# Rounding two feed-forward weights to bf16 in SBUF and turning them by DMA, with the first projections and the first LayerNorm regrouped

## The chip, the cores and the metric

One core of a Trainium2 chip runs the whole kernel. The metric is the device time of one execution in microseconds (us), taken as the median of the runs. TensorE (PE) does the matrix products, VectorE (DVE), ScalarE (ACT) and GpSimd (POOL) the rest, and SyncE (SP) issues nearly all DMAs.

## What is computed

For a batch of 8 sequences of 512 rows and 512 columns: LayerNorm, cross attention to 120 context rows with 16 heads, a residual, then a feed-forward net whose two weights are quantized to the values -1, 0 and 1 times one scale each.

```python
def weight_quant(w):
    scale = 1.0 / jnp.clip(jnp.mean(jnp.abs(w)), 1e-05)
    q = jnp.clip(jnp.round(w * scale), -1.0, 1.0) / scale
    return w + stop_gradient(q - w)
def bitlinear(x, w, b):
    return einsum('bsd,fd->bsf', act_quant(rmsnorm(x)), weight_quant(w)) + b
x = x + attn(layernorm(x), ctx, ctx, mask)      # softmax(q k^T / sqrt(32)) v, then wo
h = gelu(bitlinear(layernorm(x), w1, b1))       # w1: 2048 x 512
x = x + bitlinear(h, w2, b2)                    # w2: 512 x 2048
```

The scale needs the mean of |w| over a whole weight before any part of it can be rounded, and TensorE needs each weight turned (the contracted dimension on the partitions).

## The kernel before

**Tiles and slots.** The rows are cut into 32 tiles of 128 (k), four to a sequence (b). Every engine runs its own hand-written list of 128 slots (n), four to a tile. In slot n the softmax of one group of four heads of tile n // 4 is done: `softmax_max` on DVE (mask and negative maximum), `exps(n - 1)` on ACT, `normalize(n - 2)` on POOL, `turn_probs(n - 3)` on PE and `evac_probs(n - 3)` on ACT. `scores(n // 4)` fills four PSUM banks, ps_s, in every fourth slot. The later steps of tile k follow at fixed distances: `attend` at slot 4k + 7, `project_out` at 4k + 9, `residual` at 4k + 10, `ln2_scales` at 4k + 11, `ffn_up` from 4k + 14 on, `ffn_down` at 4k + 22. Semaphores tie the lists together; each engine works strictly in its list's order.

**A batch ahead.** TURNS and PROJ say in which slots the next sequence is prepared: "c" and "x" are turns of the context and of the four column blocks of the normalized input, "k", "v" and "q" the projections. All projections and `attend` and `project_out` share one PSUM bank, ps_a, so each waits until the last user of that bank has been read. STATS_AT and LN1_AT are the slots of LayerNorm 1, of which DVE does the statistics (`ln1_stats`) and POOL the factors and the application.

**The start.** Before slot 0 SP issues the loads, PE turns the first context and input and projects keys and the four blocks of queries of sequence 0. In `first_q` the three parts of an exact product are done one after another because wq_l comes late; `project_q` then does the other three blocks (12 matmuls each), and `evac_q` on ACT empties ps_a between them.

**The feed-forward weights** arrive in eight pieces of 128 x 2048 fp32 (p; m = p // 4 says which weight). They borrow buffers: pieces 0 and 1 hid, 2 and 3 the space of w2T, 4 that of q_hT, 5 the first four tiles of x2 (`stage`, after wo has left it), 6 and 7 hid again. What is done with each:
- `sum_abs`: four on ACT (L716, into w_abs) and four on DVE (L918).
- `total_weights` (L530, slots 1 and 7): a small matmul that sums over partitions. `weight_scales` on DVE (slots 2 and 8) makes mean, inverse and scale.
- `round_piece`: w times the inverse plus a magic number, then clipped: two passes on DVE (L925, L928) for even j, two on POOL (L1144, L1147) for odd j, in slots ROUND_AT.
- `turn_piece` on PE (L547, slots TURN_AT = 3 to 6 and 9 to 12): 16 fp32 transposes a piece, four to a bank, alternating between ps_z and ps_y; `evac_piece` on ACT (L727) and on DVE (L939) takes the magic number off and writes bf16 into w1T or w2T, two each per piece. ps_y is also the bank of the turns of TURNS.

`ffn_up` waits at its first call for w1T, `ffn_down` for w2T. SP frees the borrowed buffers in order: load_piece(6) and (7) wait for turned pieces, load_residual(2) for piece 5.

Of the kernel before, what the change touches and what calls it, by code (L numbers as in the profile page):

```python
# [27 lines left out]
def xattn_bitffn_kernel(nc, x, ctx_in, mask, wq, bq, wk, bk, wv, bv, wo, bo, w1, b1, w2, b2, out):  # L28
# [73 lines left out]
    for n in range(NU):  # L102
# [24 lines left out]
    with ExitStack() as stack:  # L127
# [30 lines left out]
        w_deq = sb("w_deq", [P, 2])  # L158

# [56 lines left out]
        names += [f"piece{p}_in" for p in range(8)]  # L216
# [40 lines left out]
        def _(sp):  # L257
# [33 lines left out]
            def slot(n):  # L291
                if n == 2:
                    sp.wait_ge(s["wo_split"], 1)
                    load_piece(5)
                if n == 4:
                    sp.wait_ge(s["wT_full"], 4)
                    load_piece(6)
                if n == 5:
                    sp.wait_ge(s["wT_full"], 8)
# [66 lines left out]
        def _(pe):  # L366
            def wait_free(use):
# [124 lines left out]
            def ffn_up(k, c):  # L492
                j = FC * k + c
                if j == 0:
                    pe.wait_ge(s["wT_act"], 16)
# [36 lines left out]
            def turn_piece(j, quarters):
                p = TURN[j]
                if j % 2 == 0:
                    pe.wait_ge(s["w_ready_dve"], j // 2 + 1)
                else:
                    pe.wait_ge(s["w_ready_pool"], j // 2 + 1)
                for q in quarters:
                    if q % 2 == 0:
                        wait(pe, "wT_act", 2 * j + q // 2)  # L540
                        bank = ps_z
                    else:
                        wait_free(Y[Y_N[("m", j, q)] - 1])
                        bank = ps_y
                    for c in range(4):
                        col = c * D + q * P if p < 4 else (4 * q + c) * P
# [690 lines left out]
```

## Time and profile before

| | us |
|---|---|
| median of 3 runs | 765.94 |
| lowest and highest of them | 760.66, 766.47 |
| the profiled execution, whole | 764.71 |
| its span, first to last instruction | 762.9 |

Mean granted TensorE clock 0.968 of full speed. The page of the profile gives each engine's busy time; the timeline and the chain of waits give the order of events, and the stretches (windows) give busy time between two instants. The span is what the rows cover; 1.8 us lie around it.

### The profile page before, as it was taken

The numbers are of one execution on the slowest core, as the hardware profiler recorded it, in microseconds if no ns is written. First come the engines' busy times: TensorE is split into PE (matmuls) and PEld (weight loads), VectorE is DVE, ScalarE is ACT, GpSimd is POOL, SyncE is SP. The second block draws the span as 40 slices with busy tenths as digits, with TensorE's granted clock in tenths as the row PEclk, the third lists the DMA queues.
The fourth block names the chain that finished last, engine by engine and source line by source line (L and its number), as shares of the span: only waits on it lengthen the run. The fifth ranks groups of instructions, "written<-read, shape, count | busy, mean of one in ns | idle before, by whom it ended". The sixth has DMA issues, their size and how long they took to land.

```text
span 762.9 us, 13877 instructions
## 1 busy us (share of the span) xinstructions
PE 666.9 (87%) x4856; PEld 428.1 (56%) x4856; DVE 604.4 (79%) x1060; ACT 521.7 (68%) x1455; POOL 505.8 (66%) x645
## 2 busy tenths in 40 slices
PE   7756778989999999999999999999999998887885
PEld 5434566656666556556655666656655664554432
DVE  3396776789788897889887978889788778888783
ACT  2254544797578778877687767877888878777360
POOL 3056343776867777777777687767777768777664
PEclk9978889999999999999999999999999999999998
DMA  9933012043322421243334332252223233232244
GB/s 308 378 123 125 12 37 69 22 104 76 76 49 57 125 51 53 64 118 76 76 63 118 76 77 57 55 122 57 54 52 74 66 63 63 63 63 64 56 77 110
DMA packets 109204, 65.37 MB, mean 86 GB/s; under 512 B 90775, under 2 KB 90775, under 8 KB 108495
## 3 DMA queue, kind: packets, MB, share of 16 engines
q1 hardware_dynamic: 108079, 64.49, 33.8%
q8 instruction: 39, 0.64, 0.3%
q14 instruction: 30, 0.25, 0.1%
q10 hardware_dynamic: 1056, 0.00, 0.1%
HBM read 35.12 MB, written 8.39 MB: 57 GB/s over the span
## 4 chain that ended last, share of the span: by engine, by line
PE 36%; DVE 35%; ACT 16%; issue 5%; DMA 4%; POOL 3%; SPq 1%; ACTq 0%; DVEq 0%; POOLq 0%
PE ps_a L405 13%; PE ps_z L507 5%; DVE hid L870 5%; DVE yw L854 5%; ACT prob L693 5%; PE ps_y L522 4%; PE ps_a L435 4%; PE ps_a L478 3%; ACT hid L700 3%; DVE yq L857 2%; PE ps_t L466 2%; DVE bn L849 2%; DVE nmax L834 2%; DVE ps_s L831 2%; DVE oT_l L799 2%
## 5 line engine op out<-in xcount | busy, mean ns | idle before, releaser
L1106 POOL TENSOR_TENSOR prob<-prob,pinv 128x480 f32<-128x480 f32 x128 | 126.3, 987 | 177.5 <-DVE pinv L839 177.5
L693 ACT ACTIVATE prob<-ps_s,nmax 128x120 f32<-128x120 f32 x512 | 180.2, 385 | 34.5 <-DVE nmax L834 34.1
L507 PE MATMUL ps_z<-w1T,q_xT 128*128 128x512 bf16 x476 | 123.9, 383 | 5.6 <-DMA q_xT<-q_x 4.5
L870 DVE SCALAR_TENSOR_TENSOR hid<-ps_z,y_deq,b_row 128x512 f32<-128x512 f32 x119 | 88.6, 744 | 45.3 <-PE ps_z L507 45.3
L693 ACT ACTIVATION_READ_ACCUMULATOR prob<-ps_s,nmax 128x1 f32 x512 | 118.2, 231 | 0.0
L522 PE MATMUL ps_y<-w2T,q_hT 128*128 128x512 bf16 x480 | 114.1, 382 | 0.3 <-DMA q_hT<-xn 0.3
L831 DVE COPY_PREDICATED_SCALAR ps_s<-hidden_key,masked_c 128x480 f32 x128 | 89.5, 700 | 16.4 <-PE ps_s L456 16.4
L466 PE MATMUL ps_t<-ident,prob 128*120 128x128 f32 x512 | 79.2, 278 | 18.0 <-ACT probT L665 10.9
L834 DVE TENSOR_REDUCE nmax<-ps_s 128x4 f32<-128x480 f32 x128 | 84.1, 657 | 4.4
L665 ACT COPY probT<-ps_t 120x512 f32<-120x512 f32 x128 | 79.5, 621 | 7.6 <-PE ps_t L466 7.2
L466 PEld LDWEIGHTS ps_t<-ident,prob 128*120 128x120 f32 x512 | 59.8, 139 | 40.4 <-ACT probT L665 21.3
L522 PEld LDWEIGHTS ps_y<-w2T,q_hT 128*128 128x128 bf16 x480 | 46.2, 99 | 62.1 <-issue 12.1
L1113 POOL TENSOR_SCALAR hid<-hid,hs 128x2048 f32<-128x2048 f32 x31 | 61.0, 1969 | 25.9 <-ACT q_h L708 18.7
L672 ACT ACTIVATE qT<-ps_a,bq_col 128x512 f32<-128x512 f32 (+1 forms) x32 | 19.7, 615 | 84.8 <-PE ps_a L405 80.5
L877 DVE TENSOR_REDUCE hs<-hid 128x1 f32<-128x2048 f32 x32 | 72.8, 2275 | 0.0
L700 ACT ACTIVATE hid<-hid 128x2048 f32<-128x2048 f32 x32 | 61.2, 1913 | 11.3 <-DVE hid L870 10.9
L507 PEld LDWEIGHTS ps_z<-w1T,q_xT 128*128 128x128 bf16 x476 | 43.0, 98 | 45.5 <-issue 13.2
L405 PE MATMUL ps_a<-xnT_h,wq_h 128*128 128x512 f32 x124 | 53.5, 431 | 15.7 <-DVE oT_l L799 11.9
L1120 POOL TENSOR_SCALAR q_h<-hid 128x2048 bf16<-128x2048 f32 x30 | 58.7, 1955 | 2.6
L405 PE MATMUL ps_a<-wo_h,oT_h 128*128 128x512 f32 x128 | 57.6, 450 | 2.4 <-DVE oT_l L799 1.4
L708 ACT ACTIVATE q_h<-hid 128x2048 bf16<-128x2048 f32 x28 | 54.2, 1937 | 0.0
L405 PE MATMUL ps_a<-wo_l,oT_h 128*128 128x512 f32 x128 | 51.4, 401 | 0.0
(155 smaller groups left out, 1397.6 us busy)
## 6 DMA issues: line engine op xcount, KB each, us to landing
xn<-in_x_dram SPq DMA_DIRECT2D x8, 1024.0 KB, 5.7
x<-in_x_dram SPq DMA_DIRECT2D x32, 256.0 KB, 2.7
out_dram<-x SPq DMA_DIRECT2D x32, 256.0 KB, 3.2
hid<-in_L_ffn_w_dram SPq DMA_DIRECT2D x4, 1024.0 KB, 8.8
w2T<-in_L_ffn_w_dram SPq DMA_DIRECT2D x2, 1024.0 KB, 14.0
ctx_k<-in_ctx_dram SPq DMA_DIRECT2D x8, 240.0 KB, 4.0
ctx_k<-in_mask_Bx1xSxS_ik_dram SPq DMA_DIRECT2D x7, 240.0 KB, 2.8
wk_s<-in_L_xattn_wk_dram SPq DMA_DIRECT2D x1, 1024.0 KB, 8.6
```

Source lines behind the costliest of these rows:

```text
L405: last = nc.tensor.matmul(bank, w, m, start=(k == 0 and i == 0), stop=(k == KD - 1 and i == 2))
L466: last = nc.tensor.transpose(ps_t[0:S2, g * P:(g + 1) * P], prob[:, n % 3, g * S2:(g + 1) * S2], ident[:])
L507: last = nc.tensor.matmul(bank[:], q_xT[:, k % 3, i], w1T[:, i, c * CH:(c + 1) * CH], start=(i == 0), stop=(i == KD - 1))
L522: last = nc.tensor.matmul(y_bank(k)[:], q_hT[:, k % 2, f], w2T[:, f], start=(f == 0), stop=(f == KF - 1))
L665: nc.scalar.copy(probT[0:S2, i], ps_t[0:S2, :].rearrange("p (g q) -> p g q", g=G)).then_inc(s["p_evac"], 1)
L693: last = nc.scalar.activation(prob[:, n % 3, g * S2:(g + 1) * S2], ps_s[n % HG][:, g * S2:(g + 1) * S2], ACT.Exp, bias=nmax[:, n % 4, g:g ...
L700: nc.scalar.activation(hid[:, k % 2], hid[:, k % 2], ACT.Gelu).then_inc(s["gelu_done"], 1)
L831: v.copy_predicated(sc, hidden_key[:, k // T % 2, k % T].unsqueeze(1).to_broadcast([P, G, S2]), masked_c[:].unsqueeze(2).to_broadcast([P, ...
L834: v.tensor_reduce(out=nmax[:, n % 4], in_=sc, op=ALU.max, axis=AX_X, negate=True).then_inc(s["sc_max"], 1)
L870: v.scalar_tensor_tensor(hid[:, k % 2, c * CH:(c + 1) * CH], z_bank(FC * k + c)[:], y_deq[:, k % 8:k % 8 + 1], b1_row[:, c * CH:(c + 1) * ...
L877: v.tensor_reduce(out=hs[:, 3, t:t + 1], in_=hid[:, k % 2], op=ALU.max, axis=AX_X, apply_absolute_value=True).then_inc(s["h_abs"], 1)
L1106: gp.tensor_tensor(pr, pr, pinv[:, n % 4].unsqueeze(2).to_broadcast([P, HG, S2]), ALU.mult).then_inc(s["prob_ready"], 1)
```

## The change

1. `round_piece` on DVE no longer multiplies and clips in fp32. It compares: w < -mean/2 into a bf16 buffer, then (w > mean/2) minus that, a `scalar_tensor_tensor`, in the same buffer w_t[:, 0] (even pieces). Odd pieces: `clip_piece` does two passes on POOL (times, min; max, plus magic), and `round_piece` on ACT takes the magic number off into w_t[:, 1] as bf16.
2. The turn of a piece is one transposing DMA from w_t (128 x 2048 bf16), issued by SP in slots TURN_W_AT. All TensorE transposes and PSUM evacuations of the weights go. w1T is stored as [P, 16, 4, 128], so that `ffn_up` reads its 512 moving columns as four runs of 128 with a step of 512 elements.
3. `first_q` and the `project_q` of sequence 0 get a bank each (ps_a, ps_s[1], ps_s[2], ps_s[3]).
4. The first input is loaded as four DMAs, and LayerNorm 1 of sequence 0 is done in halves.
5. Order: all sums of the first weight, `total_weights(0)` and `weight_scales(0)` come before slot 0; the second total is in slot 8 (it was in 7, its scales in 8). Piece 3 is loaded ahead of wv. load_piece(6) waits for round_piece(0), load_piece(7) for ACT's first rounding, load_residual(2) for ACT's third. Turns of sequence 1: 2 c, 4 to 7 x, 8 k (were 3, 5, 6, 7, 9, and 8); projections 3 k, 6 v, 9, 10, 12, 14 q (were 5, 6, 10, 12, 13, 14).

```diff
-            turns = {3: ("c", 0), 5: ("x", 0), 6: ("x", 1), 7: ("x", 2), 8: ("k", 0), 9: ("x", 3)}
-            proj = {5: ("k", 0), 6: ("v", 0), 10: ("q", 0), 12: ("q", 1), 13: ("q", 2), 14: ("q", 3)}
+            turns = {2: ("c", 0), 4: ("x", 0), 5: ("x", 1), 6: ("x", 2), 7: ("x", 3), 8: ("k", 0)}
+            proj = {3: ("k", 0), 6: ("v", 0), 9: ("q", 0), 10: ("q", 1), 12: ("q", 2), 14: ("q", 3)}
...
-    TURN = (0, 1, 2, 3, 6, 5, 7, 4)
-    ROUND_AT = (2, 2, 3, 3, 8, 8, 9, 9)
-    TURN_AT = (3, 4, 5, 6, 9, 10, 11, 12)
-    SUM_ACT_AT = {0: 2, 2: 4, 5: 6}
-    SUM_DVE_AT = {0: 3, 4: 5, 6: 7}
-    TOTAL_AT = {1: 0, 7: 1}
-    SCALES_AT = {2: 0, 8: 1}
+    SUM_ACT_AT = {6: (5,), 7: (7,)}
+    SUM_DVE_AT = {5: (4,), 6: (6,)}
+    ROUND_DVE_AT = {0: 0, 3: 2, 9: 4, 11: 6}
+    CLIP_POOL_AT = {0: 1, 5: 3, 9: 5, 11: 7}
+    ROUND_ACT_AT = {1: 1, 6: 3, 10: 5, 12: 7}
+    TURN_W_AT = {1: (0,), 2: (1,), 4: (2,), 6: (3,), 10: (4,), 11: (5,), 12: (6,), 13: (7,)}
+    TOTAL2_AT = 8
...
+        def q_bank(a, g):
+            return (ps_a, ps_s[1], ps_s[2], ps_s[3])[g] if a == 0 else ps_a
...
+            def turn_piece(p):                                   # SP
+                m, j = divmod(p, 4)
+                if m == 0:
+                    dst = w1T[:, 4 * j:4 * j + 4].rearrange("p f k q -> p (f k) q")
+                else:
+                    dst = w2T[:, :, j * P:(j + 1) * P]
+                if p % 2 == 0:
+                    sp.wait_ge(s["w_ready_dve"], p // 2 + 1)
+                    if p == 4:
+                        sp.wait_ge(s["w_ready_act"], 2)
+                else:
+                    sp.wait_ge(s["w_ready_act"], p // 2 + 1)
+                sp.dma_start_transpose(dst, w_t[:, p % 2]).then_inc(s["w_odd_in" if p % 2 else "w_even_in"], 16)
...
                 for i in range(KD):                              # ffn_up, PE
-                    last = nc.tensor.matmul(bank[:], q_xT[:, k % 3, i], w1T[:, i, c * CH:(c + 1) * CH],
+                    last = nc.tensor.matmul(bank[:].rearrange("p (f q) -> p f q", q=P), q_xT[:, k % 3, i],
+                                            w1T[:, 4 * c:4 * c + 4, i],
...
+            def round_piece(p):                                  # ACT
+                act.wait_ge(s["w_ready_pool"], p // 2 + 1)
+                wait(act, "w_odd_in", 16 * (p // 2))
+                nc.scalar.activation(w_t[:, 1], piece_buf[p], ACT.Copy, bias=-MAGIC).then_inc(s["w_ready_act"], 1)
...
-            for g in range(G):                                   # ACT, before slot 0
-                evac_q(0, g)
             sum_abs(0)
+            evac_q(0, 0)
+            evac_q(0, 1)
+            sum_abs(2)
+            evac_q(0, 2)
+            evac_q(0, 3)
...
+            def round_piece(p):                                  # DVE
+                m = p // 4
+                dve.wait_ge(s["w_stats"], 6 * m + 6)
+                dve.wait_ge(s[f"piece{p}_in"], 16)
+                wait(dve, "w_even_in", 16 * (p // 2))
+                v.tensor_scalar(w_t[:, 0], piece_buf[p], w_half[:, m, 1:2], None, ALU.is_lt).then_inc(s["w_low"], 1)
+                dve.wait_ge(s["w_low"], p // 2 + 1)
+                v.scalar_tensor_tensor(w_t[:, 0], piece_buf[p], w_half[:, m, 0:1], w_t[:, 0], ALU.is_gt, ALU.subtract
+                                       ).then_inc(s["w_ready_dve"], 1)
...
             sum_abs(1)                                           # DVE, before slot 0
+            sum_abs(3)
+            weight_scales(0)
...
+            def clip_piece(p):                                   # POOL
+                m = p // 4
+                piece = piece_buf[p]
+                pool.wait_ge(s["w_stats"], 6 * m + 6)
+                pool.wait_ge(s[f"piece{p}_in"], 16)
+                gp.tensor_scalar(piece, piece, w_inv[:, m:m + 1], 1.0, ALU.mult, ALU.min).then_inc(s["w_clip"], 1)
+                pool.wait_ge(s["w_clip"], p // 2 + 1)
+                gp.tensor_scalar(piece, piece, -1.0, MAGIC, ALU.max, ALU.add).then_inc(s["w_ready_pool"], 1)
...
-            ln1_factors(0)                                       # POOL, before slot 0
-            ln1_apply(range(2))
+            ln1_factors(0, 0, 2, 0)
+            ln1_apply((0, 1))
+            ln1_factors(0, 2, 4, 3)
```

## Rows read from the trace of the kernel before

**Rows 1.** Stretches: length, busy PE, PEld, DVE, ACT, POOL, granted clock, DMA share, GB/s
```profile
35.32:65.28 29.96, 15.37 (x78) 10.02 (x78) 23.82 (x32) 15.76 (x45) 17.44 (x13) 0.73 0.41 151
65.28:90.33 25.05, 18.64 (x151) 12.54 (x151) 17.69 (x29) 14.96 (x49) 6.61 (x8) 0.98 0.16 54
90.33:119.00 28.67, 21.32 (x168) 17.74 (x169) 21.17 (x33) 13.51 (x48) 14.22 (x10) 0.83 0.19 62
119.00:132.91 13.91, 12.44 (x90) 9.97 (x90) 7.90 (x18) 4.41 (x15) 4.09 (x7) 1.00 0.14 33
196.00:400.00 204.00, 191.16 (x1416) 123.37 (x1415) 173.35 (x309) 156.42 (x442) 150.10 (x195) 0.99 0.33 75
```
**Rows 2.** The chain of waits, 0 to 40 us: start, us, what
```profile
0.72 0.45 SPq L326
...
1.82 8.58 DMA wk_s<-in_L_xattn_wk_dram
10.45 3.71 PE ps_a L435 x8
14.18 0.59 ACT ctx_k L687
...
31.40 3.06 PE ps_a L405 x12
34.48 0.69 ACT qT L672
```
**Rows 3.** Timeline, first and last of one project_q's 12 matmuls
```profile
31.40 0.50 PE L405 MATMUL ps_a<-xnT_h,wq_h 128*128 128x512 f32 x1 [0.78 <-ACT qT L672]
...
34.06 0.39 PE L405 MATMUL ps_a<-xnT_h,wq_l 128*128 128x512 f32 x1
```
**Rows 4.** Groups by line, 30 to 134 us: busy, mean ns, idle before
```profile
L693 ACT ACTIVATE prob<-ps_s,nmax 128x120 f32<-128x120 f32 x56 | 19.5, 371 | 5.7 <-DVE nmax L834 5.7
L831 DVE COPY_PREDICATED_SCALAR ps_s<-hidden_key,masked_c 128x480 f32 x15 | 10.7, 710 | 16.2 <-PE ps_s L456 16.2
L834 DVE TENSOR_REDUCE nmax<-ps_s 128x4 f32<-128x480 f32 x15 | 9.9, 657 | 0.5
L928 DVE TENSOR_SCALAR hid<-hid 128x2048 f32<-128x2048 f32 x3 | 6.9, 2302 | 0.1
L939 DVE TENSOR_SCALAR w2T<-ps_y 128x512 bf16<-128x512 f32 x8 | 5.5, 685 | 5.7 <-PE ps_y L547 5.6
L727 ACT ACTIVATE w2T<-ps_z 128x512 bf16<-128x512 f32 x8 | 4.9, 616 | 12.2 <-PE ps_z L547 12.2
L817 DVE BATCH_NORM_STATS2 bn<-xn 128x6 f32<-128x512 f32 x8 | 5.4, 670 | 0.0
L716 ACT ACTIVATE q_h<-hid 128x2048 bf16<-128x2048 f32 x2 | 3.8, 1920 | 0.0
L980 DVE TENSOR_TENSOR wo_l<-x,wo_h 128x2048 fp32r<-128x2048 f32 x1 | 2.3, 2291 | 0.8 <-ACT wo_h L750 0.8
L1144 POOL TENSOR_SCALAR x<-x,w_inv 128x2048 f32<-128x2048 f32 x1 | 2.0, 1968 | 1.5 <-DVE w_deq L911 1.5
```
**Rows 5.** Timeline: two clipping passes on DVE, and one on POOL
```profile
49.46 2.88 DVE L928 TENSOR_SCALAR hid<-hid 128x2048 f32<-128x2048 f32 x1
51.35 2.74 POOL L1147 TENSOR_SCALAR hid<-hid 128x2048 f32<-128x2048 f32 x1
...
95.20 1.23 DVE L928 TENSOR_SCALAR hid<-hid 128x2048 f32<-128x2048 f32 x1
```
**Rows 6.** Timeline, the projection of the values of sequence 0
```profile
40.80 5.98 PE L435 MATMUL ps_a<-wv_s,ctxT 128*120 128x512 f32 x8
```
**Rows 7.** DMA issues: KB where given, median us from issue to landing
```profile
x<-in_L_xattn_wo_dram SPq DMA_DIRECT2D x1, 1024.0 KB, 13.9
...
q_hT<-q_h SPq DMA_TRANSPOSE x30, 4.3
```
**Rows 8.** Timeline, one ffn_up in the full pipeline, four matmuls
```profile
144.53 1.03 PE L507 MATMUL ps_z<-w1T,q_xT 128*128 128x512 bf16 x4
```

More of the change, by code:

```diff
@@ L158, in xattn_bitffn_kernel @@
         w_deq = sb("w_deq", [P, 2])
+        w_half = sb("w_half", [P, 2, 2])
+        w_t = sb("w_t", [P, 2, F], BF16)
         xn = sb("xn", [P, T, D])
@@ L215, in xattn_bitffn_kernel @@
             z_full z_evac gelu_done sq_done h_abs h_scales h_magic qh_ready h_rms hdeq_ready y_full y_evac last_magic qh_last""".split()
-        names += [f"piece{p}_in" for p in range(8)]
+        names += [f"piece{p}_in" for p in range(8)] + [f"first{t}_in" for t in range(T)]
         names += [f"res{i}_in" for i in range(XR)] + [f"out{i}" for i in range(XR)]
@@ L294, in slot @@
                     load_piece(5)
[L295 to L299, printed above, removed]
+                    sp.wait_ge(s["w_ready_act"], 1)
                     load_piece(7)
+                for p in TURN_W_AT.get(n, ()):
+                    turn_piece(p)
                 k = tile_at(n, YOUT0)
@@ L324, in slot @@
                     sp.dma_start(ctx_s, ctx_in[b]).then_inc(s["ctx_in"], 16)
-            sp.dma_start(xn[:], x_v[0]).then_inc(s["x_in"], 16)
+            for t in range(T):
+                sp.dma_start(xn[:, t], xt_v[0, t]).then_inc(s[f"first{t}_in"], 16)
             sp.dma_start(ctx_s, ctx_in[0]).then_inc(s["ctx_in"], 16)
@@ L331, in _ @@
             sp.dma_start(mask0_in, mask_v[0]).then_inc(s["mask_in"], 16)
-            for p in range(3):
+            for p in range(4):
                 load_piece(p)
             sp.dma_start(wv_s[:], wv.rearrange("(k p) n -> p k n", p=P)).then_inc(s["wv_in"], 16)
-            load_piece(3)
             wait(sp, "turn_full", YT_N[("k", 0, 0)] + 1)
@@ L528, in total_weights @@
                 pe.wait_ge(s["abs_dve"], 2 * (m + 1))
-                wait(pe, "wT_act", 8 * m)
+                wait(pe, "w_stats", 6 * m)
                 nc.tensor.matmul(ps_z[:, 0:4], ones, w_abs[:, m], start=True, stop=True).then_inc(s["w_sum"], 1)
[L532 to L546, printed above, removed]
-                        last = nc.tensor.transpose(bank[:, c * P:(c + 1) * P], piece_buf[p][:, col:col + P], ident[:])
-                    last.then_inc(s["wT_full"], 1)
             def slot(n):
@@ L672, in evac_q @@
                 last = nc.scalar.activation(qT[:, first:first + whole, g],
-                                            ps_a[:, 0:whole * P].rearrange("p (t q) -> p t q", q=P),
+                                            q_bank(a, g)[:, 0:whole * P].rearrange("p (t q) -> p t q", q=P),
                                             ACT.Identity, bias=bq_col[:, g:g + 1], scale=SCALE)
@@ L757, in slot @@
                     square_h(k)
-                if n in SUM_ACT_AT:
-                    sum_abs(SUM_ACT_AT[n])
+                for p in SUM_ACT_AT.get(n, ()):
+                    sum_abs(p)
+                if n in ROUND_ACT_AT:
+                    round_piece(ROUND_ACT_AT[n])
                 k = tile_at(n, GELU0)
@@ L815, in ln1_stats @@
             def ln1_stats(a, t):
-                wait(dve, "x_in", 16 * (a + 1))
+                if a == 0:
+                    dve.wait_ge(s[f"first{t}_in"], 16)
+                else:
+                    dve.wait_ge(s["x_in"], 16 * a)
                 v.bn_stats(out=bn1[:, t], in_=xn[:, t]).then_inc(s["ln1_part"], 1)
@@ L1162, in slot @@
                     h_factor(k)
-                for j in range(1, 8, 2):
-                    if n == ROUND_AT[j]:
-                        round_piece(j)
+                if n in CLIP_POOL_AT:
+                    clip_piece(CLIP_POOL_AT[n])
                 k = tile_at(n, B20)
```

123 lines of the change are left out of this document (40 added, 83 removed).

## The prediction

> **What bounds the kernel now.** I read the stretches first, then the chain of waits, then the groups and the timeline. From 196 to 400 us, which stands for the long middle, PE is busy 191.2 of 204.0 us [rows 1]; the reader is to see that the middle is full, and that the change touches nothing there but the way in which ffn_up reads w1T. The first 14 slots are different. From scores(0) at 35.32 to ffn_up(0) at 132.91 pass 97.6 us, with PE busy 67.8 and DVE 70.6 of them [rows 1]: no engine is full, the slots are a relay between engines, and the weights' work lies in that relay. Four slots take 30.0, 25.1 and 28.7 us there, though no feed-forward is yet running, where the 114 slots after ffn_up(0) take (762.9 - 132.9) x 4 / 114 = 22.1 per four, the drain at the end included. The granted clock of TensorE is 0.73 in the first stretch and 0.83 in the third [rows 1]: PE waits long enough to fall to its lower level, and then its work takes longer.
>
> Before slot 0 the chain of waits goes through wk's landing at 10.40, the keys' projection (3.71 us), ACT's copy of the keys at 14.18, and later a loop of a 3.06 us projection and a 0.69 us evacuation [rows 2].
>
> All sums below are made against the profiled execution (span 762.9, whole 764.7), which lies 1.2 us under the median of the runs.
>
> **The first LayerNorm in halves: 0.** It could bring the input's turns forward by up to the one us that PE idles before them, but the chain enters through wk and ACT's copy of the keys at 14.18 [rows 2], and ACT must do that copy before it takes the first turned block. The early input waits there. If that cover were gone, the gain would be some 2 us (two tiles of statistics, each 0.67 and its aggregate [rows 4]). Three more DMA issues, 0.45 each [rows 2], come ahead of wk's, 1.4 us of SP time; wk moves behind the same megabyte of x in the same DMA engines, so I take 0. The bounds are 0 and +1.4.
>
> **A bank each: -2.8.** In one block the last of 12 matmuls starts 2.66 us after the first, so a block free of waits takes 2.66 x 12/11 = 2.9 [rows 3]. The loop of before is 3.06 + 0.02 + 0.69 + 0.04 = 3.8 [rows 2]. Three loops lose 0.9 each, 2.8. The sums of pieces 0 and 2 (ACT, 1.92 [rows 4]) now stand between the evacuations; they fit, since a block takes 2.9 and an evacuation 0.7. Piece 3 lands one megabyte earlier, and both DVE sums (2.3 each) end near 28 to 30; PE's total follows the last block at 31.6, so it should find its inputs there. scores(0) starts at about 32.5 instead of 35.3.
>
> **Slots 0 to 3: 30.0 becomes 25.0.** DVE's list loses one sum (2.3), the small scale steps (0.6), four fp32 passes (between 1.23 alone and 2.88 blocked [rows 5], 2.30 in L928's mean [rows 4]) and two evacuations (0.69 each [rows 4]). It gets two roundings. The comparison is a one-input pass of 2048 elements from SBUF, nearest to L928 alone, 1.23 [rows 5]. The second step reads two tensors in SBUF, nearest to wo_l, 2.29 [rows 4]. The bounds of that are 1.23 and 2.88; I take 2.29, thus 3.5 a piece. The block also stays: beside a POOL pass L928 took 2.88 instead of 1.23 and ended 2.88 after it began, with POOL's own pass at 2.74 instead of 1.97 [rows 4, 5]. I let them take turns.
>
> The walk is this. DVE masks (0.71 + 0.66, 1.35 with overlap [rows 4]) until 35.1. POOL clips piece 1 from 32.9 to 36.8 (2 x 1.97), so DVE's rounding ends at 36.8 + 1.2 + 2.3 = 40.3. Mask 1 ends at 41.6. wo is issued just before block 1 of the queries starts (23.7, two loops of 3.8 before 31.40), so it lands 13.9 later [rows 7], about 36, when ACT comes to it; ACT's cast of it is a pass like L716's, so wo_l ends at 43.9, two tiles' statistics at 45.5, mask 2 and two more tiles at 48.6, the values' bias at 49.3. Only now may PE use ps_a for the keys of sequence 1 in slot 3. PE finished the values at 33.7 + 3.7 and has been nearly idle since, so this projection costs what the values' did after such an idle, 5.98 and not 3.7 [rows 2, 6]; it ends at 55.4. ACT's list has evac_keys ahead of exps(3), so exps(3) (56 such in 19.5 us, 1.4 for four [rows 4]) ends at 57.4 and scores(1) starts at 57.5, before 65.3. Rounding piece 2 is hidden in that wait.
>
> **Slots 4 to 7: 25.1 becomes 21.** Gone are PE's turns of pieces among the projections and their evacuations (0.62 on ACT, 0.69 on DVE [rows 4]). DVE: two masks, one turned block's low part, sum of piece 4 to 64.4; mask, low part, sum of piece 6 to 68.7; the values' bias waits for the projection, which I take at the low clock, 64.2 to 70.2. Mask 7 ends at 72.3. ACT: sum of piece 5 and rounding of piece 3 (1.92 each) to 70, then block 2, exps(6), attend's copy, probT, sum of piece 7 to 76.3, block 3, exps(7) to 78.2. scores(2) starts at 78.3, before 90.3. It is ACT that ends last here.
>
> **Slots 8 to 11, and the first ffn_up.** q0, w0, q1 take 3.7 (low clock at first), 2.9, 2.9 with evacuations between. DVE's rounding of piece 4 stands against POOL's clip of piece 5: 3.5 + 3.9 in turns from 82.9 to 90.4. The same happens in slot 11, 93.9 to 101.4; the statistics of LayerNorm 2, the mask of sequence 1 and oT_low(1) follow until 104.9, and only then may PE start q2. scores(3) itself starts at 100.8, before 119.0. q2 (2.9), its evacuation (1.0), w1 (2.9) and the residual bring ffn_up(0) to 112.2, before 132.9. The sum: 2.8 + 5.0 + 4.2 + 6.2 + 2.5 = 20.7.
>
> **The DMAs of the turns: 0.** A transposing DMA of 128 x 2048 bf16 lands 4.3 after its issue [rows 7]. ffn_up(0) needs the first four, long done; ffn_down(0) is eight slots off. What waits is the next rounding into the same half of w_t. Only that of piece 6 is close: turn 4 issued at 90.4 lands at 94.7, rounding wanted at 93.9, 0.8 in a stretch where DVE is last. On SP turn 5 waits for ACT's third rounding near 97, and ahead of it load_residual(2) and the input of sequence 2 wait for the same; that input lands at about 103, wanted at 106. Behind turn 6 is turn_x(0), wanted at 105.5: later by one issue at most. Hidden but thin; bounds 0 to +3.
>
> The Trainium skill (DMA: Bandwidth & Descriptors, Latency and other measured facts) says that a transposing DMA with a non-contiguous middle dimension loses some 30% of its bandwidth, which the w2 pieces' destination has. By it, as an estimate, turn 4 would land near 96 and the total would be 1.3 us longer. No row here shows such a destination.
>
> **ffn_up's four runs: 0.** Four matmuls took 1.03 [rows 8]; PE may read the 128-column runs as fast as one. Nothing in the trace has such a moving operand. The lower bound is 0; the upper is a rival below.
>
> **Sum.** My walk leaves out the short hand-overs between engines, and most waits are taken at their best, so I keep 20 of 20.7: 764.7 - 20 = 745 for a profiled execution; 745 also for the median, which lies about one us higher in before.
>
> **Rivals.** (a) Forecast, gain kept, 738 to 753: 0.72. The upper end adds the bounds named above (1.4, 3) and 4 for projections at the low clock that I took at the high one (2.3 each), the lower takes away one blocked pass per piece.
> (b) The second rounding step is not held up by POOL and the clock stays high: the two low-clock projections lose 2.3 each and four roundings lose about 1.5 each, 745 - 8 = 737. Speaking for it: no row shows a pass with two SBUF inputs beside a POOL pass. Against: L928 was held [rows 5] and PE's idle time before slot 3 is nine us. 0.08. The Trainium skill (SBUF — State Buffer, Who interferes with whom) has a DVE instruction with two SBUF inputs contend with a POOL instruction that reads SBUF, whoever comes second waiting for the whole of the other; by it the walk's turns stand and (b) fails.
> (c) The relay eats half: with the weights' transposes gone from the same stretch the clock stays low through slots 4 to 12 (0.73 is seen in the first [rows 1]), so q0, w0, q1, q2, w1 take 5 instead of 2.9 and DVE waits for them; 5 x 2.1, all of it on the path, gives 755. For it: the clock was 0.83 even with the transposes. Against: the projections themselves warm it. 0.12.
> (d) Slower: ffn_up reads each run as a matmul of its own. It decides in the middle, where PE is 94% busy. If the four runs cost 25% more, 1.03 / 4 = 0.26 [rows 8] grows by 0.065, and 32 x 4 x 4 = 512 matmuls by 33 us: 778. Above 0.04 us a matmul it eats the gain. For it: nothing shows such a read. Against: the elements within a run are contiguous. 0.05.
> (e) No change: the head start is given back later, since a DMA or a stall fixed in time sets the middle. DMA share in the middle is 0.33 [rows 1], so hardly. 763 to 766. 0.03.
>
> About 1% is what a measurement of this kernel can tell from no change. Faster by over 1% (under 758): (a), (b), (c), 0.90 with a little of (c) lost; within: (e) and a mild (d), 0.06; slower: 0.04. The range 737 to 756 holds (a), (b) and (c) in part; it leaves out about 2 in 10.
>
> **What would show each step.** scores(0) starts near 32.5; one project_q follows the other with no idle. The keys' projection in slot 3 starts near 49 and takes 6; scores(1), (2), (3) near 57, 78, 101 and ffn_up(0) near 112; comparison 1.2, second step 2.3, more beside POOL; ACT's rounding 1.9; weight DMAs land within 6. The time from ffn_up(0) to the end stays at 630 and four ffn_up matmuls 1.03. If scores(1) to ffn_up(0) come as said and the end doesn't, the fault is in the middle; if ps_a's users in slots 9 to 13 take 5 us each, it is (c).

## The result and the profile after

The changed kernel took 775.03 us (median of 4 runs, 773.50 to 776.18) and the kernel before 766.21 (4 runs): a ratio of 1.012, with an interval of 1.008 to 1.016. It is a little slower, where 745 was forecast. All times are medians over a kernel's executions; one of the four of experiment 8 ran at a granted clock of 0.65, took 940.55 us and is left out. The profiled execution took 773.5 us, of which the span is 771.7. The 8.8 us more against the profiled 764.7 of before arise in the first 143 us: ffn_up(0) starts 10.1 later, and 1.3 come back behind it. From ffn_up(0) to the end pass 771.7 - 143.0 = 628.7 us, against 762.9 - 132.9 = 630.0 before and 630 in the forecast.

The stretches of the changed kernel, from scores(0) to scores(1), to scores(2), to ffn_up(0), and the long middle (length, busy PE, PEld, DVE, ACT, POOL, granted clock, DMA share, GB/s; they answer to [rows 1]):

```profile
33.01:64.01 31.00, 11.91 (x60) 6.05 (x61) 26.97 (x26) 11.05 (x38) 23.63 (x11) 0.72 0.80 235
64.01:91.24 27.23, 14.04 (x106) 8.65 (x107) 14.42 (x26) 15.99 (x47) 21.03 (x9) 0.80 0.26 61
91.24:142.98 51.74, 29.82 (x188) 23.44 (x189) 44.20 (x40) 16.76 (x56) 40.05 (x17) 0.71 0.40 84
196.00:400.00 204.00, 193.87 (x1469) 126.10 (x1468) 174.89 (x319) 160.09 (x451) 154.50 (x201) 1.00 0.32 76
```

The middle is as full as before. In the first three stretches POOL is the surprise: 23.6 us busy in the first, 21.0 in the second (6.6 before, in the stretch that answers to it) and 40.1 in the third, with PE busy 38 to 58% of each. The chain of waits of the changed kernel, 0 to 130 us (start, us, what), says which work it is:

```profile
33.01 1.20 PE ps_s L472 x32
...
35.66 5.73 DVE w_t L926
41.41 6.49 DVE w_t L928
...
67.83 7.14 POOL w2T L1135
75.06 7.09 POOL w2T L1137
...
96.66 7.52 DVE w_t L926
104.20 6.47 DVE w_t L928
110.69 4.25 DMA w2T<-w_t
115.07 7.77 DVE w_t L926
122.86 6.46 DVE w_t L928
```

Eight of these are steps of DVE and POOL, 54.7 us, on the path: two of clip_piece (L1135, L1137) and six of round_piece (L926, L928). The timeline shows how they hang together (start, us, engine, line, operation, out<-in, idle time before and its releaser):

```profile
33.12 7.17 POOL L1135 TENSOR_SCALAR hid<-hid,w_inv 128x2048 f32<-128x2048 f32 x1 [17.05 <-DVE w_deq L911]
40.38 7.97 POOL L1137 TENSOR_SCALAR hid<-hid 128x2048 f32<-128x2048 f32 x1
...
35.66 5.72 DVE L926 TENSOR_SCALAR w_t<-hid,w_half 128x2048 bf16<-128x2048 f32 x1
41.41 6.49 DVE L928 SCALAR_TENSOR_TENSOR w_t<-hid,w_half,w_t 128x2048 bf16<-128x2048 f32 x1
...
57.88 1.28 DVE L926 TENSOR_SCALAR w_t<-w2T,w_half 128x2048 bf16<-128x2048 f32 x1
59.19 2.35 DVE L928 SCALAR_TENSOR_TENSOR w_t<-w2T,w_half,w_t 128x2048 bf16<-128x2048 f32 x1
```

A clipping pass of POOL takes 7.17 us, not 1.97. DVE's comparison takes 1.28 with no POOL pass beside it, but 5.72 when it begins inside such a pass, and it ends at 41.38, 1.1 us after the pass does. The second step takes 2.35 alone and 6.49 inside. So a slow pass is paid twice: by whoever needs the clipped piece, and by whatever DVE has to do meanwhile.

The starts of the slots in the profiled executions, in us, with the forecast's walk and the kernel of experiment 1 beside them (the 132.9 of before is the chain's instant, which the forecast used; its row in the timeline starts at 132.75):

| | scores(0) | scores(1) | scores(2) | ffn_up(0) | span less ffn_up(0) |
|---|---|---|---|---|---|
| before | 35.3 | 65.3 | 90.3 | 132.9 | 630.0 |
| forecast | 32.5 | 57.5 | 78.3 | 112.2 | 630 |
| after | 33.0 | 64.0 | 91.2 | 143.0 | 628.7 |
| experiment 1 (e1_pool_pairs) | 32.9 | 56.4 | 74.6 | 110.8 | 631.3 |

### The profile page after: what moved, and what is told of

Its sections match the earlier page's. It is cut to its first block, busy times and chain, and to the rows that moved or that the text cites. A ratio compares the mean times of both kernels' runs of the same rounds, so it can differ in the third digit from the quotient of the medians.

```text
span 771.7 us, 13605 instructions
## 1 busy us (share of the span) xinstructions
PE 654.9 (85%) x4728; PEld 417.7 (54%) x4728; DVE 620.5 (80%) x1048; ACT 521.3 (68%) x1443; POOL 549.4 (71%) x648
## 4 chain that ended last, share of the span: by engine, by line
DVE 36%; PE 35%; ACT 13%; POOL 6%; issue 5%; DMA 4%; SPq 1%; ACTq 0%; DVEq 0%; POOLq 0%
PE ps_a L421 12%; PE ps_z L524 6%; DVE hid L867 5%; DVE yw L851 5%; PE ps_y L541 4%; PE ps_a L494 4%; ACT prob L691 4%; PE ps_a L451 3%; ACT hid L698 3%; DVE w_t L926 3%; PE ps_t L482 3%; DVE yq L854 3%; DVE w_t L928 3%; DVE bn L846 2%; DVE oT_l L793 2%
## 5 line engine op out<-in xcount | busy, mean ns | idle before, releaser
L691 ACT ACTIVATE prob<-ps_s,nmax 128x120 f32<-128x120 f32 x512 | 180.7, 386 | 36.8 <-DVE nmax L831 36.4
L482 PE MATMUL ps_t<-ident,prob 128*120 128x128 f32 x512 | 80.9, 282 | 45.1 <-POOL prob L1097 28.0
L670 ACT ACTIVATE qT<-ps_a,bq_col 128x512 f32<-128x512 f32 (+1 forms) x29 | 17.7, 609 | 89.3 <-PE ps_a L421 87.0
L421 PE MATMUL ps_a<-xnT_h,wq_h 128*128 128x512 f32 x112 | 50.1, 447 | 28.9 <-DVE oT_l L793 20.4
L698 ACT ACTIVATE hid<-hid 128x2048 f32<-128x2048 f32 x32 | 61.2, 1912 | 10.8 <-DVE hid L867 10.5
L421 PE MATMUL ps_a<-wo_h,oT_l 128*128 128x512 f32 x128 | 51.5, 402 | 0.0
## 6 DMA issues: line engine op xcount, KB each, us to landing
hid<-in_L_ffn_w_dram SPq DMA_DIRECT2D x4, 1024.0 KB, 10.2
```

What stands on the lines that cost most here:

```text
L421: last = nc.tensor.matmul(bank, w, m, start=(k == 0 and i == 0), stop=(k == KD - 1 and i == 2))
L482: last = nc.tensor.transpose(ps_t[0:S2, g * P:(g + 1) * P], prob[:, n % 3, g * S2:(g + 1) * S2], ident[:])
L691: last = nc.scalar.activation(prob[:, n % 3, g * S2:(g + 1) * S2], ps_s[n % HG][:, g * S2:(g + 1) * S2], ACT.Exp, bias=nmax[:, n % 4, g:g ...
L698: nc.scalar.activation(hid[:, k % 2], hid[:, k % 2], ACT.Gelu).then_inc(s["gelu_done"], 1)
```

## The experiments

The theory after the result: all of the loss is POOL's choice of operations. The old code scaled with the pair (multiply, add) and clipped with (min, max); the new one uses (multiply, min) and (max, add). Its rivals: the rounding on DVE, the transposing DMAs or the clock eat the gain, and the slow passes of POOL are only seen in their company.

**1. The changed kernel with POOL's old pairs.** Both pairs leave the piece scaled, clipped, rounded and with MAGIC added; all else is the changed kernel.

```diff
-gp.tensor_scalar(piece, piece, w_inv[:, m:m + 1], 1.0, ALU.mult, ALU.min).then_inc(s["w_clip"], 1)
+gp.tensor_scalar(piece, piece, w_inv[:, m:m + 1], MAGIC, ALU.mult, ALU.add).then_inc(s["w_clip"], 1)
-gp.tensor_scalar(piece, piece, -1.0, MAGIC, ALU.max, ALU.add).then_inc(s["w_ready_pool"], 1)
+gp.tensor_scalar(piece, piece, MAGIC + 1.0, MAGIC - 1.0, ALU.min, ALU.max).then_inc(s["w_ready_pool"], 1)
```

> The changed kernel with one edit: on POOL, clip_piece uses the pairs of operations of before (multiply, add; then min, max) in place of (multiply, min; then max, add). Theory A, the new pairs of operations are slow on POOL (7.1 us a pass against 1.97) and hold DVE up through the SBUF they share: passes of 2.0, DVE's comparison 1.3 to 3, its second step 2.3 to 4, scores(1) near 57 and ffn_up(0) near 112 to 115, in all 742 to 750 us. Rival B, the passes are slow through where they stand (DVE or DMA traffic beside them): they stay at 7 and the time at 775. Rival C, the pairs are only part of it, and the low clock or the DMAs of the turns cost the rest: passes of 2.0 but 755 to 765.

Measured: 742.93 us against 763.78 of before on the same chip, 0.971 (0.968 to 0.975). Two lines give 32 us back (775.03 to 742.93; about 31 by the two ratios, 29.6 between the spans). Its timeline:

```profile
32.97 1.97 POOL L1135 TENSOR_SCALAR hid<-hid,w_inv 128x2048 f32<-128x2048 f32 x1 [17.07 <-DVE w_deq L911]
35.02 1.89 POOL L1137 TENSOR_SCALAR hid<-hid 128x2048 f32<-128x2048 f32 x1
...
35.50 2.49 DVE L926 TENSOR_SCALAR w_t<-hid,w_half 128x2048 bf16<-128x2048 f32 x1
38.02 2.35 DVE L928 SCALAR_TENSOR_TENSOR w_t<-hid,w_half,w_t 128x2048 bf16<-128x2048 f32 x1
...
82.43 3.85 DVE L928 SCALAR_TENSOR_TENSOR w_t<-q_hT,w_half,w_t 128x2048 bf16<-128x2048 f32 x1
```

DVE's four roundings sum to 44.0 us in the changed kernel and to 21.1 here, a difference of 22.9; POOL's clip of piece 3, for which ACT waits 8.4 and behind which POOL's next pass over the probabilities stands in the chain, takes 14.3 there and 3.9 here, a difference of 10.4. Together that is 33.3, beside the 32.2 by which ffn_up(0) starts earlier. By instants the loss lies in all three stretches: 7.6 us at scores(1), 9.0 more at scores(2), 15.6 more at ffn_up(0).

**2. The kernel before with the new pairs.** The same exchange the other way, eight passes in `before`, nothing else.

```diff
-gp.tensor_scalar(piece, piece, w_inv[:, m:m + 1], MAGIC, ALU.mult, ALU.add
+gp.tensor_scalar(piece, piece, w_inv[:, m:m + 1], 1.0, ALU.mult, ALU.min
-gp.tensor_scalar(piece, piece, MAGIC + 1.0, MAGIC - 1.0, ALU.min, ALU.max
+gp.tensor_scalar(piece, piece, -1.0, MAGIC, ALU.max, ALU.add
```

> The kernel before with one edit: its four POOL roundings use the pairs of operations of the change (multiply, min; then max, add), which give the same numbers. Theory A: each pass takes 7.1 instead of 1.9 to 3.0, DVE's roundings beside them are held up as well, slots 2, 3, 8 and 9 lengthen, 785 to 800 us. Rival B: no change, 764 to 768.

Measured: 807.47 against 763.78, 1.056 (1.051 to 1.060), more than I expected. Eight passes at 5.2 more each make 41.6 of the 43.7 us, and ffn_up(0) starts 42.9 later (175.6 against 132.8 in the timeline), so there is next to no cover. I had counted on some. The timeline shows a reason, since DVE's own clipping pass of the other piece stands still meanwhile, 8.09 us where 1.23 is its price alone [rows 5]:

```profile
48.30 8.26 POOL L1144 TENSOR_SCALAR hid<-hid,w_inv 128x2048 f32<-128x2048 f32 x1 [0.84 <-DVE w_deq L911]
49.55 8.09 DVE L928 TENSOR_SCALAR hid<-hid 128x2048 f32<-128x2048 f32 x1
```

So the slow passes need neither the new rounding nor the transposing DMAs; the pair alone makes them.

**3. Experiment 1 with the first input whole.** It undoes the first LayerNorm in halves: one DMA of x, one computation of the factors for all four tiles.

```diff
-            for t in range(T):
-                sp.dma_start(xn[:, t], xt_v[0, t]).then_inc(s[f"first{t}_in"], 16)
+            sp.dma_start(xn[:], x_v[0]).then_inc(s["first0_in"], 16)
...
-            ln1_factors(0, 0, 2, 0)
+            ln1_factors(0, 0, 4, 0)
             ln1_apply((0, 1))
-            ln1_factors(0, 2, 4, 3)
...
```

> e1 with the first input loaded by one DMA again and LayerNorm 1 of sequence 0 done in one go. If the halves bring nothing since the chain enters through wk, and three more issues put wk off by 0.8 us: wk lands at 10.4 instead of 11.2, scores(0) starts 0.8 earlier and the whole is 0 to 1 us shorter than e1. If the early input helps: 1 to 2 us longer than e1.

Measured: 742.74, 0.972 (0.968 to 0.975), beside 742.93 with halves. The halves bring nothing, as forecast. The chains of both kernels show both sides of it: whole, wk's landing ends nothing, the keys' projection starts at 10.77 and scores(0) at 32.45; in halves the projection waits for wk until 11.13 and scores(0) starts at 32.86.

**4. The price of POOL's passes by themselves.** A kernel that leaves the whole computation out and only times passes of 128x2048 fp32: on POOL alone for nine pairs of operations, on DVE alone, then both together.

```diff
+gp.tensor_scalar(b[:], a[:], one[:, 0:1], MAGIC, ALU.mult, ALU.add)           # L42
+gp.tensor_scalar(b[:], a[:], MAGIC + 1.0, MAGIC - 1.0, ALU.min, ALU.max)      # L46
+gp.tensor_scalar(b[:], a[:], one[:, 0:1], 1.0, ALU.mult, ALU.min)             # L50
+gp.tensor_scalar(b[:], a[:], -1.0, MAGIC, ALU.max, ALU.add)                   # L54
+gp.tensor_scalar(b[:], a[:], one[:, 0:1], 1.0, ALU.mult, ALU.mult)            # L58
+gp.tensor_scalar(b[:], a[:], one[:, 0:1], 1.0, ALU.add, ALU.add)              # L62
```

> A kernel of its own that leaves the whole computation out and only times passes over 128 x 2048 fp32. POOL alone, each pair of operations twice; then DVE alone (comparison to bf16, and the two-input second step); then both side by side. Theory A: (mult, add) 1.97 and (min, max) 1.90, (mult, min) and (max, add) 7.1, with no DVE and no DMA near; DVE alone 1.28 and 2.35. Beside a POOL pass the comparison waits until that pass ends. The second step either waits as well, or runs along slowly (6.46 against 2.35 was seen beside a slow pass, and it ended before that pass did). Rival B: all POOL pairs 1.9 to 2.0 alone.

Measured (timeline, one line for each of those pairs, with POOL alone):

```profile
6.40 1.98 POOL L42 TENSOR_SCALAR b<-a,one 128x2048 f32<-128x2048 f32 x1 [5.59 <-DMA a<-in_x_dram]
...
10.54 1.89 POOL L46 TENSOR_SCALAR b<-a 128x2048 f32<-128x2048 f32 x1
...
14.51 7.17 POOL L50 TENSOR_SCALAR b<-a,one 128x2048 f32<-128x2048 f32 x1
...
29.03 7.09 POOL L54 TENSOR_SCALAR b<-a 128x2048 f32<-128x2048 f32 x1
...
43.38 1.97 POOL L58 TENSOR_SCALAR b<-a,one 128x2048 f32<-128x2048 f32 x1
...
47.52 7.17 POOL L62 TENSOR_SCALAR b<-a,one 128x2048 f32<-128x2048 f32 x1
```

The pairs (multiply, add), (min, max) and (multiply, multiply) take 1.9 to 2.0 us. The pairs (multiply, min), (max, add), (add, add), (min, min), (max, multiply) and (greater, multiply) take 7.1 to 7.2. Each was run twice, with the same times within 0.02. It is thus not min or max or add that is slow, since each of them stands in a fast pair too: three of the nine pairs are fast. Nor is it the operands: (multiply, min) in L50 and (multiply, multiply) in L58 read the same tile and have the same two operands, and take 7.17 and 1.97. What divides the pairs inside POOL isn't shown by these runs.

The second half of the same timeline has DVE beside POOL:

```profile
107.73 2.35 DVE L122 SCALAR_TENSOR_TENSOR w<-c,one,w 128x2048 bf16<-128x2048 f32 x1
...
114.89 3.94 DVE L129 SCALAR_TENSOR_TENSOR w<-c,one,w 128x2048 bf16<-128x2048 f32 x1
116.80 3.88 POOL L81 TENSOR_SCALAR b<-a,one 128x2048 f32<-128x2048 f32 x1
...
128.72 7.09 POOL L88 TENSOR_SCALAR b<-a 128x2048 f32<-128x2048 f32 x1
128.73 6.63 DVE L137 SCALAR_TENSOR_TENSOR w<-c,one,w 128x2048 bf16<-128x2048 f32 x1 [1.94 <-POOL b L85]
...
165.55 7.08 POOL L104 TENSOR_SCALAR b<-a 128x2048 f32<-128x2048 f32 x1
165.57 8.14 DVE L157 TENSOR_SCALAR w<-c,one 128x2048 bf16<-128x2048 f32 x1 [1.94 <-POOL b L101]
```

Alone the second rounding step takes 2.35. Beside fast passes it and they take turns, 3.94 and 3.88 each. Beside a slow pass it takes 6.63 and ends at 135.36, 0.45 before the pass does. The comparison (L157) takes 8.14 beside a slow pass and ends 1.08 after it, with 1.28 as its price alone (1.28 in L118's row too). These are the 6.49 and the 7.5 of the changed kernel.

**5. Experiment 1 with the first queries in one bank.**

```diff
         def q_bank(a, g):
-            return (ps_a, ps_s[1], ps_s[2], ps_s[3])[g] if a == 0 else ps_a
+            return ps_a
...
             def project_q(a, g):
-                bank = q_bank(a, g) if a == 0 else a_bank(("q", a, g))
+                bank = a_bank(("q", a, g))
```

(a_bank is what makes each block wait until the bank has been read.)

> e1 with all four blocks of queries of sequence 0 back in ps_a (one bank, waits between them). The prediction's term says 3 loops of 0.9 us: scores(0) 2.8 us later than in e1 (32.9 becomes 35.6), and the whole 2 to 3 us longer than e1, about 745 to 746. Rival: the later start is swallowed, since DVE and POOL meet wo's landing and the waits of slots 0 to 2 anyway: 743 as e1.

Measured: 745.64, 0.973 (0.969 to 0.976). In the profile scores(0) starts at 35.44 and not at 32.86, 2.6 later. But wk landed 0.5 earlier here (10.56 against 11.09); counted from the start of the keys' projection, scores(0) comes after 24.84 us against 21.73. The term is thus 3.1, where the forecast said 2.8. The timeline has the last of its three loops, ACT's evacuation after a wait for a whole block:

```profile
34.61 0.69 ACT L670 ACTIVATE qT<-ps_a,bq_col 128x512 f32<-128x512 f32 x1 [3.16 <-PE ps_a L421]
```

ffn_up(0) comes 2.1 later (112.94 against 110.82). The medians differ by 2.7, but the intervals of the two ratios overlap, so the instants carry this verdict, not the times.

**6. Experiment 1 with idle transposes on PE, to keep the clock up.** It tests rival (c), that the low clock in the first 14 slots eats the gain. The transposes read the identity and write a part of ps_z that nobody uses then.

```diff
+            FILL = {2: 60, 5: 12, 7: 8, 8: 12, 11: 20, 12: 6}
+
+            def fill(n):
+                for _ in range(FILL.get(n, 0)):
+                    nc.tensor.transpose(ps_z[:, P:2 * P], ident[:], ident[:])
...
+                if n in (5, 7, 8, 11, 12):
+                    fill(n)
...
+                if n == 2:
+                    pe.wait_ge(s["w_stats"], 6)
+                    fill(n)
```

> e1 with idle transposes of the identity into an unused part of ps_z (60 in slot 2, 12, 8, 12, 20, 6 in slots 5, 7, 8, 11, 12), so that PE does not fall to its lower clock while it waits. If the low clock costs what the prediction put on it (the two projections 5.1 and 5.3 instead of 3.7, scores 2.1 instead of 1.2 twice): 3 to 5 us less than e1, 738 to 740. If those stretches are covered by DVE and ACT: as e1. If the fillers stand in the way of the turns: up to 3 us more.

Measured: 740.41, 0.966 (0.961 to 0.970), no different from experiment 1 within the intervals. As a test of the clock it was only half of one: the transposes of slot 2 ended at 44.94, 4.6 us before the keys' projection, and that still took 5.39 us. But the block q2, 12 matmuls from 100.38 on, took 3.08 us where experiment 1 has 5.49, and ffn_up(0) started at 108.92, 1.9 before experiment 1. Experiment 10 repeats it with more in slot 2.

**7. Experiment 1 with the slow pairs for piece 3 alone.** Piece 3 is the one whose passes stand in the chain themselves.

```diff
-                gp.tensor_scalar(piece, piece, w_inv[:, m:m + 1], MAGIC, ALU.mult, ALU.add).then_inc(s["w_clip"], 1)
+                if p == 3:
+                    gp.tensor_scalar(piece, piece, w_inv[:, m:m + 1], 1.0, ALU.mult, ALU.min).then_inc(s["w_clip"], 1)
+                else:
+                    gp.tensor_scalar(piece, piece, w_inv[:, m:m + 1], MAGIC, ALU.mult, ALU.add).then_inc(s["w_clip"], 1)
```

(and likewise for the second pass)

> e1 with the slow pairs of operations for piece 3 alone, the one piece clipped on POOL with no rounding on DVE beside it. If the slow pairs cost the kernel in two ways, by delaying what is queued behind them on POOL (normalize) and by holding DVE, then this piece shows the first alone: 14.2 instead of 3.9 us of POOL, some 8 to 10 us more than e1, 751 to 753; the other three pieces are then worth the remaining 20 or so. If POOL's delay is hidden and only the holding of DVE costs: as e1.

Measured: 752.80, 0.982 (0.978 to 0.986). That is some 10 us over experiment 1 (0.982 - 0.971, of 767, makes 8; the medians differ by 9.9, the starts of ffn_up(0) by 10.3), as expected. Of the 10.3, 1.3 are there at scores(0) already, before any weight is clipped. The stretch from scores(1) to scores(2), in which piece 3 is clipped, takes 27.3 us against 18.2, thus 9.0 more, the same as in the changed kernel: of two passes at 5.2 more each, nearly all shows.

**8. Experiment 1 with the slow pairs for piece 5 alone.** Piece 5's clip stands beside DVE's rounding of piece 4. The edit is that of experiment 7 with `p == 5`.

> e1 with the slow pairs of operations for piece 5 alone, whose two POOL passes run beside DVE's rounding of piece 4. By the trace of the changed kernel DVE's two steps then take 7.5 and 6.5 where e1 has 2.3 and 3.9, which is 7.8 us on DVE's list, and DVE ends last there: 6 to 8 us more than e1, 749 to 751. With e6 (9 to 10 for piece 3) and two more pieces like this one the sum is 30 to 33, the whole distance between e1 and the changed kernel. If it gives under 3 us, DVE's being held is covered and the distance must come from elsewhere.

Measured: 753.17, 0.982 (0.978 to 0.986), thus 10 to 12 us over experiment 1 and its repetition, experiment 9, and not the 6 to 8 that I expected. The timeline has DVE's two steps as expected, and one thing that I had left out:

```profile
79.06 7.17 POOL L1136 TENSOR_SCALAR x<-x,w_inv 128x2048 f32<-128x2048 f32 x1
86.32 7.97 POOL L1141 TENSOR_SCALAR x<-x 128x2048 f32<-128x2048 f32 x1
...
79.79 7.52 DVE L926 TENSOR_SCALAR w_t<-q_hT,w_half 128x2048 bf16<-128x2048 f32 x1
87.34 6.49 DVE L928 SCALAR_TENSOR_TENSOR w_t<-q_hT,w_half,w_t 128x2048 bf16<-128x2048 f32 x1
...
94.49 0.80 PE L421 MATMUL ps_a<-xnT_h,wq_h 128*128 128x512 f32 x1 [8.46 <-DVE x L841]
```

Both DVE steps are held up, each by a pass of its own, 14.0 us where experiment 1 has 2.34 + 3.85 = 6.2, thus 7.8 more. What I had left out is PE. It waits 8.46 us for the residual that DVE computes behind these steps, and then its block q1 takes 5.43 us (94.49 to 99.92) where experiment 1 has 3.07 after a wait of 0.75: 2.4 more, at a granted clock of 0.52 against 1.00. The two make 10.2, and the stretch from scores(2) to ffn_up(0) takes 46.3 us against 36.2, 10.1 more. So of the 32 us, by the instants of the changed kernel, piece 1 has 7.6, piece 3 has 9.0, and pieces 5 and 7 together have 15.6; piece 5 alone costs 10.1. A slow pass of piece 1 or 7 alone was not run.

**9. Experiment 1 again, in more rounds, as the partner of experiment 10.** No edit.

> e1 again, for a comparison on one chip with the next kernel: ratio to the kernel before 0.97.

Measured: 741.62 against 766.38, 0.968 (0.965 to 0.972).

**10. More idle transposes.** The edit of experiment 6 with 82 in slot 2 in place of 60.

> e5 with 82 idle transposes in slot 2 in place of 60, so that they reach to the first probabilities' turn at 47 and the keys' projection at 49.5, which in e5 still took 5.4, takes 3.7. By the price of the low clock: 1 to 2 us less than e5, 738 to 740, and 3 to 5 less than e1. If the projection keeps 5.4, as e5.

Measured: 740.97, 0.967 (0.964 to 0.969), on the chip of experiment 9. This time the clock stayed up until 100 us. The windows of experiment 9 and then of this one, 40 to 100 us:

```profile
40.00:100.00 60.00, 36.75 (x274) 25.78 (x274) 49.56 (x69) 35.37 (x117) 32.79 (x25) 0.79 0.55 141
```

```profile
40.00:100.00 60.00, 45.37 (x401) 35.94 (x399) 50.55 (x73) 34.74 (x117) 32.74 (x25) 0.97 0.59 151
```

The granted clock is 0.97 instead of 0.79, and the keys' projection takes 3.69 us:

```profile
49.65 3.69 PE L451 MATMUL ps_a<-wk_s,ctxT 128*120 128x512 f32 x8 [1.74 <-DVE v_s L811]
```

Yet ffn_up(0) starts at 110.92 against 111.09. Up to 100 us the low clock is nearly hidden: the block q2 starts at 100.74 against 102.02, 1.3 earlier, of which 0.55 is wk's earlier landing. DVE, busy 49.6 and 50.6 of the 60 us, hardly changes its pace, and PE's projections wait for it either way. What is not hidden is q2 itself. It took 5.49 us here at a granted clock of 0.50, 4.38 in experiment 9, 5.49 in experiment 1 and 3.08 in experiment 6 at 1.00, and from its start to ffn_up(0) passed 10.18, 9.07, 10.20 and 8.54. So the low clock at q2 costs up to 1.7 us, which the medians can't tell from nothing. Rival (c) had five blocks at 5 us on the path, 10.5 us; in experiment 1 they took 3.53, 3.06, 3.07, 5.49 and 3.09, so it came about in one of the five.

## Why the prediction was wrong

**The step that failed** is one term in the walk of slots 0 to 3, used again in slots 8 to 11: "POOL clips piece 1 from 32.9 to 36.8 (2 x 1.97)". The 1.97 is L1144's [rows 4], a pass of the same engine, shape and types, but of another pair of operations: (multiply, add), while the new code has (multiply, min) and (max, add). The diff shows the exchange in its two lines. I gave the exchange no sentence of its own, let alone bounds, though no row of before has either pair. It measured 7.16 and 7.09. So the clip of a piece is 14.3 us instead of 3.9.

**The step built on it** also failed in size: "3.5 + 3.9 in turns". The mechanism was right, since DVE is held up. But two steps of DVE beside two slow passes take 14.0 us together, 7.5 for the comparison and 6.5 for the second step, against 7.4 in the sum.

**The rest of the sum stands** as a whole, as experiment 1 shows, with single stretches off by up to 2.6 us. It has every other part of the change and measured 742.93 and, again, 741.62, against 745 forecast:

- LayerNorm in halves, 0: right within what experiment 3 can tell. wk was issued at 3.12 in the changed kernel and landed at 11.24, 0.8 later than before, inside the bounds. But with the same code up to there the keys' projection, which waits for it, started anywhere from 10.60 (experiment 5) to 12.15 (experiment 9), so the 0.8 can't be put down to the halves.
- A bank each, -2.8: 3.1. From the start of the keys' projection to scores(0) pass 24.87 us before and 24.84 in experiment 5, and 21.73 in the changed kernel and in experiment 1. scores(0) itself came only 2.3 earlier than before (33.0), since wk landed later.
- Slots 0 to 3: wo_l was to end at 43.9 and ended at 43.9 in experiment 1; the values' bias at 49.3 and ended at 49.1; the keys' projection was to start at 49.3 at the low clock and take 5.98, and took 5.08 from 49.18; scores(1) 57.5, measured 56.4.
- Slots 4 to 7: scores(2) 78.3, measured 74.6. This is the worst of the instants, put 3.7 too late, 1.1 of it from the stretch before. The values' projection, walked from 64.2 to 70.2, ran from 62.0 to 67.3.
- Slots 8 to 11: scores(3) 100.8, measured 96.5; ffn_up(0) 112.2, measured 110.8. The stretch from scores(2) to ffn_up(0) is 2.3 longer than in the walk, so two errors cancel in part, and that the total came out so near is partly luck. The chief term behind the 2.3 is q2, put at 2.9: PE did little from 92.0 on, and q2 took 5.49 at the low clock.
- The comparison was put at 1.23 and took 1.28; the second step at 2.29, and took 2.35; ACT's rounding at 1.92, and took 1.91 to 1.94. The block of a two-input step by a fast POOL pass, which no row of before had, is real (3.94).
- The DMAs of the turns: the one wait foreseen, 0.8 for piece 6, was 1.03 in experiment 1. The changed kernel has it as well, behind the 4.25 us DMA piece of its chain.
- ffn_up from four runs: 1.03 us for four matmuls in experiment 1, and a mean of 386 ns for one in the changed kernel's groups against 383 before (383 in experiment 1 as well). Rival (d) is out.
- Rival (e) is out as well: in experiment 1 ffn_up(0) comes 22.1 us earlier, and the span is 20.8 shorter. The 1.3 between them are no more than the scatter of that part: from ffn_up(0) to the end pass 628.7 to 632.7 us in the changed kernel and the experiments, 630.0 before.

The changed kernel's DMA issues (KB where given, median us from issue to landing) are these:

```profile
w1T<-w_t SPq DMA_TRANSPOSE x4, 6.0
w2T<-w_t SPq DMA_TRANSPOSE x4, 5.0
```

The w2 pieces with their scattered destination landed sooner than the w1 pieces, not later. The 30% that the Trainium skill (DMA: Bandwidth & Descriptors, Latency and other measured facts) takes off such a transfer isn't seen here; the DMA queue carried other traffic at the same time, so these two rows are no clean comparison. None of the w1 turns lay on the path.

Rival (b)'s first half fell: the second step is held up. So did its second: the clock was low at the keys' projection (5.08). The Trainium skill (SBUF — State Buffer, Who interferes with whom) has the later of the two wait for the whole of the other. The trace agrees for fast passes and for the comparison; beside a slow pass the second step ended 0.45 us before the pass, so there the measurement and not the rule decides.

Why were no bounds there? The walk asked for each operation "which row is nearest" and took engine, shape and type as the measure of near. On DVE and ACT that served within 4%. On POOL it was off by 3.6 times. No row of before could have given 7.1. But POOL's pass over the probabilities, another operation, has a row in both profiles; in the changed kernel's groups by line it is

```profile
L1097 POOL TENSOR_TENSOR prob<-prob,pinv 128x480 f32<-128x480 f32 x128 | 126.4, 988 | 126.8 <-DVE pinv L836 126.8
```

and 2048 elements at its 988 / 480 = 2.06 ns make 4.2 us. That bound, from a row however far, would have been 2.25 over the value taken; the 5.2 that a pass really costs more made 32 us, so it would have added about 14 us to the upper end, to 770, past the time of before and still short of the 775 measured. And the trace of before did show that POOL's time hangs on the pair, in rows that I passed over (groups by line, before):

```profile
L1096 POOL TENSOR_SCALAR y_deq<-yq,w_deq 128x1 f32<-128x1 f32 x32 | 9.8, 307 | 3.7
...
L1087 POOL TENSOR_SCALAR yq<-mv 128x1 f32<-128x1 f32 x32 | 6.1, 190 | 2.7
```

L1096 is (max, multiply) and L1087 (multiply, add), on one column each: 307 ns against 190. L1096 also reads its second factor from a tile; with two constants in both, (add, multiply) on four columns took 306 ns (L1057) and (multiply, add) 198 (L1060). How much a pass of 2048 columns would cost they don't say: (add, multiply) on 512 columns took 781 ns (L1065) beside 688 for (multiply, add) (L1075). What could have been seen blind is thus that the two lines changed their operations, that nothing priced them, and that DVE's time hung on the same term.

## What to carry to other kernels

Price an instruction from a row with the same operations, not only the same engine, shape and type; on POOL the pair alone moved a 128x2048 pass from 1.9 us to 7.2. Where a diff swaps the operations of a pass, treat that as a part of the change with bounds of its own, and try the old pair before anything else: here two lines turn a kernel at 775 us into one at 742 to 743, 3% under the kernel before. And a slow POOL pass costs DVE's time too, so a POOL pass that looks hidden isn't if DVE is in the same relay.

## What the runs showed of the hardware that was not expected

- POOL's tensor_scalar on 128x2048 fp32 has two prices, 1.9 to 2.0 us and 7.1 to 7.2, set by the pair of operations (experiment 4).
- Beside a slow POOL pass the comparison waits until the pass is over (8.14 us, ends 1.08 after it), but the two-input step ends 0.45 before it (6.63). Why it may, these runs don't say.
- In the other direction a POOL pass of 7.09 was drawn out to 8.79 when a DVE step had begun 0.5 us before it: that step ends at 137.75, and 7.09 more make 144.8, close to the pass's end at 144.69. The timeline of experiment 4:

```profile
135.40 2.35 DVE L139 SCALAR_TENSOR_TENSOR w<-c,one,w 128x2048 bf16<-128x2048 f32 x1
135.90 8.79 POOL L90 TENSOR_SCALAR b<-a 128x2048 f32<-128x2048 f32 x1
```

- A granted clock of 0.79 and one of 0.97 over the 60 us from 40 to 100 gave the same start of ffn_up(0) within 0.2 us (experiments 9 and 10), while a single block of 12 matmuls on the path took 5.49 us at the low clock and 3.08 at the high one (q2 in experiments 1 and 6).
- A held-up DVE step can cost PE's clock too: after a wait of 8.46 us behind it, a block took 5.43 us instead of 3.07 (experiments 8 and 1).
- wk's one megabyte took 7.46 us from issue to landing in experiment 5 and 9.00 in experiment 9, with the same DMAs ahead of it.
